# Blocks of 256 rows with four buffers each, in place of blocks of 512 rows with two, in the routed experts of a fused kernel

## The reference, cut to what matters

```python
# h: [8192, 128] tokens after the second layer norm; 8 experts, 2 of them per token
probs = sigmoid(h @ router_w.T + routing_bias)
scores, idx = top_k(probs, 2); scores = scores / scores.sum(-1)     # w: scores at idx
g = silu(einsum('th,ehi->tei', h, gate_w)); u = einsum('th,ehi->tei', h, up_w)
combined = einsum('tei,eih,te->th', g * u, down_w, w)               # routed experts, I = 256
shared = silu(h @ shared_gate.T) * (h @ shared_up.T) @ shared_down.T
x = x + gb * (shared + combined)
```

## Time and profile before

| | |
|---|---|
| time, median of 3 runs | 1456.23 us (1455.55 to 1457.21) |
| the profiled execution: its time, its span in the profile | 1459.87 us, 1458.1 us |
| first load of the block stage issued (SP) | at 1076.5 us of the span |
| last rows of the block stage loaded (SP) | at 1346.0 us |
| first load of the step stage issued (SP) | at 1376.4 us |
| TensorE busy, whole span | 89% |
| TensorE busy from 1100 to 1340 us | 185.7 of 240 us |

### The profile page before, as it was taken

The page is one execution under the profiler, slowest core; times in us unless marked ns, Lnnn a source line. Parts: engine busy times, 40 slices in busy tenths (PEclk is TensorE's granted clock), DMA queues, the critical chain, the costliest instruction groups (busy, mean ns, idle before and its releaser), DMA issues.

```text
span 1458.1 us, 38072 instructions
## 1 busy us (share of the span) xinstructions
PE 1298.9 (89%) x10935; PEld 1072.5 (74%) x10935; DVE 1094.8 (75%) x3120; ACT 812.4 (56%) x2061; POOL 927.0 (64%) x1426
## 2 busy tenths in 40 slices
PE   6999999999999999999999999999138767787796
PEld 5888788888888788888878888787027656676686
DVE  8888889898898988989898998987133433433387
ACT  5666666666666666666666676665023333333342
POOL 3444776867677686776867677676725555555555
PEclk9999999999999999999999999999559988989898
DMA  8902020202112020220202112020224434443154
GB/s 240 259 7 81 2 96 0 95 16 78 40 55 95 6 89 20 75 90 5 95 15 80 34 61 95 4 92 23 103 81 125 130 114 125 122 124 117 50 168 144
DMA packets 94721, 118.46 MB, mean 81 GB/s; under 512 B 9668, under 2 KB 60535, under 8 KB 94672
## 3 DMA queue, kind: packets, MB, share of 16 engines
q1 hardware_dynamic: 85584, 100.93, 22.1%
q0 software_dynamic: 9088, 16.94, 3.5%
HBM read 50.13 MB, written 61.08 MB: 76 GB/s over the span
## 4 chain that ended last, share of the span: by engine, by line
PE 50%; DVE 22%; issue 13%; SPq 7%; POOL 2%; DMA 2%; DVEq 1%; ACT 1%; another core or an unknown queue 1%; POOLq 0%; ACTq 0%
PE head_banks L1394 10%; PE bank L1405 8%; PE bank L1415 6%; DVE pairs L1048 5%; PE bank L1318 5%; PE bank L1319 5%; PE bank L1320 5%; DVE pairs L1044 4%; DVE A L1070 3%; DVE pairs L1053 2%; SPq L384 2%; PE bank L1356 2%; PE bank L1357 2%; PE bank L1358 2%; DVE xn L887 1%
## 5 line engine op out<-in xcount | busy, mean ns | idle before, releaser
L635 POOL DMA_INDIRECT y_dram<-pairs,y_row x156 | 155.0, 994 | 147.3 <-issue 124.9
L1318 PE MATMUL bank<-h_hi,big 128*128 128x256 f32 x768 | 237.2, 309 | 3.4 <-DVE h_lo L895 2.8
L1044 DVE TENSOR_TENSOR_SCAN pairs<-pairs 128x128 f32<-128x128 f32 x512 | 232.2, 494 | 4.4 <-issue 1.7
L1394 PE MATMUL head_banks<-pairs 64*128 64x128 f32 x2048 | 225.9, 297 | 5.3 <-DVE A L1070 3.2
L1405 PE MATMUL bank<-A,shared 128*64 128x256 f32 (+1 forms) x2048 | 223.0, 339 | 0.0
L1048 DVE TENSOR_TENSOR_SCAN pairs<-pairs,cap 128x128 f32<-128x128 f32 x512 | 219.8, 469 | 0.0
L1319 PE MATMUL bank<-h_lo,big 128*128 128x256 f32 x768 | 216.8, 282 | 0.0
L1320 PE MATMUL bank<-h_hi,big 128*128 128x256 f32 x768 | 216.4, 282 | 0.0
L463 POOL TENSOR_SCALAR_AFFINE_SELECT A<-A 128x256 f32<-128x256 f32 x256 | 113.7, 444 | 154.5 <-ACT A L744 153.4
L1394 PEld LDWEIGHTS head_banks<-pairs 64*128 64x128 f32 x2048 | 155.6, 186 | 62.6 <-issue 42.5
L1070 DVE COPY_PREDICATED A<-causal,head_banks 128x384 f32<-128x384 int32 x256 | 150.2, 587 | 63.4 <-PE head_banks L1394 62.2
(11 more groups left out here) (193 smaller groups left out, 2816.3 us busy)
## 6 DMA issues: line engine op xcount, KB each, us to landing
rows_dram<-pad_row SPq DMA_DIRECT2D x17, 2080.0 KB, 8.2
pairs<-rows_dram SPq DMA_DIRECT2D x39, 260.0 KB
pairs<-y_dram SPq DMA_DIRECT2D x16, 512.0 KB, 3.8
pairs<-in_L_ffn_gate_w_dram SPq DMA_DIRECT2D x39, 128.0 KB
pairs<-in_L_ffn_up_w_dram SPq DMA_DIRECT2D x39, 128.0 KB
pairs<-in_L_ffn_down_w_dram SPq DMA_DIRECT2D x39, 128.0 KB
token_rows<-new_rows SPq DMA_DIRECT2D x16, 260.0 KB, 2.3
mod_rows<-mod_rows_dram SPq DMA_DIRECT2D x32, 128.0 KB, 3.2
```

Source lines behind the costliest of these rows:

```text
L635: g.indirect_dma_start(y_dram, bass.IndirectOffsetOnAxis(ap=y_row[:, u, n:n + 1], axis=0), y_out[:, u, n, :], None, bounds_check=TOKENS * ...
L1044: v.tensor_tensor_scan(F[:, par, cols], ga_t[:, par, cols], ga_t[:, par, cols], 1.0, ALU.mult, ALU.min)
L1318: t.matmul(dst, hi, m_hi, start=True, stop=False)
L1394: last = t.matmul(S[:, h, c * P:(c + 1) * P], keys[rows, :], queries[rows, :], start=True, stop=True)
```

## The change

The routed experts' rows are cut into blocks of 256 rows, of which there are 2 * 8192 / 256 + 7 = 71. Every tile that a block loads or stores (`erows`, `ew_in`, `ed_in`, `y_out`, `y_known`, `y_row`) has four buffers, each with a semaphore of its own. The split weights, the split rows and PSUM keep two (`half` in the code). SP's loads run further ahead: rows, gate and up of block i+6 are issued where before it was i+2, down of block i+4 where it was i+1. To make room, `erows` and `ed_in` move into `ga_all`, which is not used by then. GpSimd issues two scatters per block. The loops over blocks are written out four blocks at a time. The step stage still has 512 tokens a step. Some semaphores of other parts are merged, to free eight for the new buffers.

```diff
-BLOCKS = TOP * TOKENS // STEP + E - 1
+BLOCK = 256
+BT = BLOCK // P
+RING = 4
+BLOCKS = TOP * TOKENS // BLOCK + E - 1
...
+        after = ga_all[:, :, :].rearrange("p b d -> p (b d)")
+        erows = after[:, 0:RING * BT * ROW].rearrange("p (u n c) -> p u n c", u=RING, n=BT)
+        ed_in = after[:, 3072:4096].rearrange("p (u i d) -> p u i d", u=RING, i=IT)
...
+        TURNS = (BLOCKS - 3) // RING
+
+        def unit(k, j):
+            return k * RING + j, j % RING, j % 2, k + j // RING
+
+        def begun(turn):
+            return not (isinstance(turn, int) and turn == 0)
...
-            def load_rows(i, u):
-                if not (isinstance(i, int) and i < 2):
-                    alone(s_hx, i - 1)
-                    alone(s_yr, i - 1)
+            def load_rows(k, j):
+                i, u, _, turn = unit(k, j)
+                if begun(turn):
+                    alone(s_hx, i - (RING - 1))
+                    alone(s_yr, i - (RING - 1))
...
-            def load_ahead(i, u):
-                load_rows(i + 2, u)
-                load_gate_up(i + 2, u)
-                load_down(i + 1, 1 - u)
...
+            with sp.Fori(0, TURNS - 1) as k:
+                for j in range(RING):
+                    load_rows(k, j + RING + 2)
+                    load_gate_up(k, j + RING + 2)
+                    load_down(k, j + RING)
...
-                for n in range(ST):
+                for n in range(BT):
                     g.indirect_dma_start(y_dram, bass.IndirectOffsetOnAxis(ap=y_row[:, u, n:n + 1], axis=0),
                                          y_out[:, u, n, :], None, bounds_check=TOKENS * TOP - 1,
                                          oob_is_err=False).then_inc(s_ysc[u], 16)
...
-                if not (isinstance(k, int) and k == 0):
-                    alone(s_ysc[u], k * 64)
+                if begun(turn):
+                    alone(s_ysc[u], turn * 16 * BT)
                 v.tensor_copy(y_row[:, u, :], y_known[:, u, :]).then_inc(s_id, 1)
...
+            def turn_of_blocks(k):
+                for j in range(RING):
+                    rows_transposed(k, j + 2)
+                    gate_up_block(k, j + 1)
+                    down_block(k, j)
```

More of the change, by code:

```diff
@@ L239, in block_kernel @@
         s_tab, s_blk = sem("table_step"), sem("table_ready")
-        s_rin, s_win, s_din, s_ysc, s_yin = ([sem(f"{n}_{u}") for u in range(2)] for n in (
-            "rows_in", "weights_in", "down_in", "y_scattered", "y_loaded"))
+        s_rin, s_win, s_din, s_ysc = ([sem(f"{n}_{u}") for u in range(RING)] for n in (
+            "rows_in", "weights_in", "down_in", "y_scattered"))
+        s_yin = [sem(f"y_loaded_{u}") for u in range(2)]
         s_hx, s_ehh, s_ehl, s_ewh, s_ewl = (sem(n) for n in (
@@ L384, in expert, with load_gate_up @@
                 return sp.value_load(block_i[0:1, 1, ds(i, 1)], min_val=0, max_val=E - 1)
-            def load_rows(i, u):
-                if not (isinstance(i, int) and i < 2):
-                    alone(s_hx, i - 1)
-                    alone(s_yr, i - 1)
[L390 to L395, removed]
+            def load_rows(k, j):
[3 more added lines that the diff above has]
+                    alone(s_yr, i - (RING - 1))
+                row = sp.value_load(block_i[0:1, 0, ds(i, 1)], min_val=0, max_val=ROWS - BLOCK)
+                sp.dma_start(erows[:, u, :, :], rows_dram[ds(row, BLOCK), :].rearrange("(p n) c -> p n c", p=P)).then_inc(s_rin[u], 16)
+            def load_gate_up(k, j):
+                i, u, _, turn = unit(k, j)
+                if begun(turn):
+                    alone(s_ewl, i - (RING - 1))
                 e = expert(i)
@@ L398, in load_gate_up, with load_down @@
                 sp.dma_start(ew_in[:, u, I:2 * I], up_w[ds(e, 1), :, :].rearrange("e h i -> h (e i)")).then_inc(s_win[u], 16)
-            def load_down(i, u):
-                if not (isinstance(i, int) and i < 2):
-                    alone(s_dn, i - 1)
+            def load_down(k, j):
+                i, u, _, turn = unit(k, j)
+                if begun(turn):
+                    alone(s_dn, i - (RING - 1))
                 e = expert(i)
                 sp.dma_start(ed_in[:, u, :, :], down_w[ds(e, 1), :, :].rearrange("e (i p) d -> p (e i) d", p=P)).then_inc(s_din[u], 16)
[L406 to L409, removed]
-            def load_ahead(i, u):
-                load_rows(i + 2, u)
-                load_gate_up(i + 2, u)
-                load_down(i + 1, 1 - u)
[L416 to L425, removed]
+            for i in range(RING):
+                load_rows(0, i)
+                load_gate_up(0, i)
+                if i >= 1:
+                    load_down(0, i - 1)
+            load_down(0, RING - 1)
+            for i in (RING, RING + 1):
+                load_rows(0, i)
+                load_gate_up(0, i)
+            with sp.Fori(0, TURNS - 1) as k:
[3 more added lines that the diff above has]
+                    load_down(k, j + RING)
+            for j in range(3):
+                if j < 1:
+                    load_rows(TURNS - 1, j + RING + 2)
+                    load_gate_up(TURNS - 1, j + RING + 2)
+                load_down(TURNS - 1, j + RING)
+            for u in range(RING):
+                sp.wait_ge(s_ysc[u], 16 * BT * len(range(u, BLOCKS, RING)))
             sp.wait_ge(s_dn, BLOCKS)
@@ L616, in _ @@
                 with pool.Fori(0, B) as b:
-                    alone(s_fmv, b + 1)
-                    g.tensor_scalar(veps[:, :], mv[:, :, 1], EPS, None, ALU.add).then_inc(s_fve, 1)
-                    alone(s_fve, b + 1)
+                    alone(s_fmv, b * 2 + 2)
+                    g.tensor_scalar(veps[:, :], mv[:, :, 1], EPS, None, ALU.add).then_inc(s_frs, 1)
+                    alone(s_frs, b * 2 + 1)
                     g.tensor_tensor(rstd[:, :], veps[:, :], neg_half[:, 0:CHUNKS], ALU.pow).then_inc(s_frs, 1)
@@ L637, in scatter_y @@
                                          oob_is_err=False).then_inc(s_ysc[u], 16)
[L639 to L642, removed]
+            with pool.Fori(0, TURNS) as k:
+                for j in range(RING):
+                    scatter_y(k, j)
+            for j in range(3):
+                scatter_y(TURNS, j)
             pool.wait_ge(s_gb, 16)
@@ L803, in high_h_shared, with silus, copy_y_out @@
                 a.activation(eh_hi[:, u, :], h_all[:, ds(j * STEP, STEP)], ACT.Copy).then_inc(s_ehh, 1)
[L805 removed]
+            def silus(v, width):
                 for i in range(IT):
                     sc.wait_ge(s_g, v * 2 + i + 1)
[L808 to L810 removed]
+                    a.activation(silu[:, i, 0:width], GU[i][0][:, 0:width], ACT.Silu).then_inc(s_silu, 1)
+            def copy_y_out(k, j):
+                v, u, half, turn = unit(k, j)
@@ L811, in copy_y_out @@
                 sc.wait_ge(s_dn, v + 1)
[L812 to L838, removed]
+                if begun(turn):
+                    sc.wait_ge(s_ysc[u], turn * 16 * BT)
+                a.activation(y_out[:, u, :, :], DN[half][:, 0:BT * D].rearrange("p (n d) -> p n d", n=BT), ACT.Copy).then_inc(s_yo, 1)
@@ new lines, in _ @@
+            for j in range(2):
+                high_weights(0, j)
+                high_h(0, j)
+            silus(0, BLOCK)
+            def turn_of_blocks(k):
+                for j in range(RING):
+                    high_weights(k, j + 2)
+                    high_h(k, j + 2)
+                    silus(k * RING + j + 1, BLOCK)
+                    copy_y_out(k, j)
+            turn_of_blocks(0)
+            with sc.Fori(1, TURNS) as k:
+                turn_of_blocks(k)
+            high_weights(TURNS, 2)
@@ L913, in _ @@
                 last = v.tensor_scalar(mod[:, k, :], ps, float(k % 2), None, ALU.add)
-            last.then_inc(s_mod, 1)
+            last.then_inc(s_cm, 1)
             dve.wait_ge(s_rows_ps, 1)
@@ L1227, in gate_times_up, with y_rows, y_rows_out @@
                     alone(s_u, m * 2 + i + 1)
-                    v.tensor_tensor(act[:, u, i, :], GU[i][1][:, :], silu[:, i, :], ALU.mult).then_inc(s_act, 1)
-            def y_rows(m, u, k):
-                alone(s_rin[u], k * 16 + 16)
-                if not (isinstance(k, int) and k == 0):
-                    alone(s_id, m - 1)
+                    v.tensor_tensor(act[:, u, i, 0:width], GU[i][1][:, 0:width], silu[:, i, 0:width], ALU.mult).then_inc(s_act, 1)
+            def y_rows(k, j):
+                m, u, _, turn = unit(k, j)
+                alone(s_rin[u], turn * 16 + 16)
+                if begun(turn):
+                    alone(s_id, m - (RING - 1))
                 v.scalar_tensor_tensor(y_known[:, u, :], erows[:, u, :, D + 1], block_e[:, ds(m, 1)], erows[:, u, :, D],
                                        ALU.not_equal, ALU.add).then_inc(s_yr, 1)
-            def y_rows_out(m, u, k):
+            def y_rows_out(k, j):
+                m, u, _, turn = unit(k, j)
                 alone(s_yr, m + 1)
-                if not (isinstance(k, int) and k == 0):
```

(44 more changed lines are left out.)

204 lines of the change are left out of this document (94 added, 110 removed).

## The result

The changed kernel takes 1514.6 us (median of 4 runs, 1513.9 to 1515.3) where the kernel before took 1455.9 us in the same job: a ratio of 1.0401 [1.0383, 1.0419], 59 us slower. I had forecast slower, at 1559 us. In the profiles the difference is 54 us, since the profiled execution of the kernel before took 1459.87 us, 4 us more than its median. Numbers in fences are start and duration in us unless a sentence says otherwise.

The account below looks back on a forecast made before the run. SP's instruction queue was taken to bound the block stage: 1099 + 64 x 5.65 + 0.9 = 1461.5, plus 18 us, starts the step stage 103 us later; 1456.2 + 103 = 1559 us. Range 1500 to 1620 us.

Parts of the forecast that it names:

- SP's queue paces the changed kernel, so more blocks cost time: Block stage: SP's own instructions set the pace at 5.65 us a block, 71 blocks in place of 39; 75%.
- The first rival: Block stage: the buffers were the bound, so GpSimd paces the new stage at 3.5 us a block, 1422 us; 5%.
- The number: Whole kernel: median of 1559 us, 103 us later than before.
- the second rival: Block stage: SP paces, but short scatter groups don't slow it; 4.22 us a block, 1468 us; 11%.
- the scatters' cost to SP: Block stage: SP's instructions slow beside scatters, 0.71 us per scatter, 1.42 us a block for two.
- SP's quiet work: Block stage: SP's instructions for one block without scatter slowdown, counted as 4.22 us in the changed kernel.
- SP sets the pace of the kernel before, too: Block stage before the change: SP's rows loads every 7.32 us are the stage's pace, with some 12 us of waits.
- the third rival: Block stage: SP's slowdown goes with the block, not the scatters; 6.84 us a block, 1635 us; 8%.
- Other engines, DMA, the step stage: Other engines at most 3.5 us a block, DMA some 150 us hidden in about 400, step stage unchanged at 82 us.
- The signs: New profile: loads 5.65 us apart, SP without waits, 0.7 us pieces beside scatter pairs, TensorE under 77%, cast not released by scatters.

## Why the prediction was right, and where it was off

*SP's queue paces the changed kernel, so more blocks cost time.* Right, and shown in three ways: SP never waits, an unused read costs its full time, and a load moved off SP gives back 89 us. The first rival (GpSimd at 3.5 us a block, 1422 us) is out. Whether SP serves three loads a block or four decides 6% of the time.

In the prediction I held the rule of the Trainium skill ("DMA: Bandwidth & Descriptors", section "Issuing engines are not separate DMA queues"), that starting a DMA is usually small beside the DMA, for refuted by the trace. Taken load by load the trace agrees with it: where SP is quiet, it issues a rows load in 0.33 us, and the rows land 2.1 us after the issue. What does not follow from it is that SP can't be the bound. The four issues are only 1.4 of SP's 4.51 us a block, and the rest is three table reads (not the two I named: the expert is read twice), register operations and waits that are met at once.

*The number* is 44 us off, and 1514.6 us lies outside the 1532 to 1592 us that I gave the forecast itself; it lies in the stated 1500 to 1620 because that range reached towards the second rival.

*The term that was mis-sized is the scatters' cost to SP*: 1.42 us for a pair. It comes to 4.97 - 4.51 = 0.46 us, with the pace measured on the chip of the result and the quiet work on two others; SP's quick instructions have the same medians on both kinds of chip (333 ns for the gate load, 384 for the down load, 0.27 us for the instruction that reads a word of the table). The same kernel with its scatters took 4.55 us a block on a quiet chip, which gives 0.42. I had divided the loss beside four scatters by four. It isn't proportional: the second rival, that a short group hardly slows SP, was nearer. As I had priced it, 1468 us, it missed by as much as the forecast did. With the measured quiet work it comes to 1099 + 64 x 4.51 + 18.9 = 1406.5 for the end of the block stage, 30 us later than before, or 1486 us.

*SP's quiet work* was counted 0.29 us short (4.22, measured 4.51), which hid part of the other error. It made part of it, too: what I did not count as SP's own work in the kernel before I put down to its scatters. With the quiet work 0.29 us longer, four scatters cost an estimated 6.95 - 4.62 = 2.3 us (4.51, and 0.11 more for the loop end of that kernel) and a pair in proportion 1.2, and the pace would again have been forecast at 5.7 us. So the luck is small, and it is the proportion that failed. The measured pace is 0.68 us lower than forecast, 44 us over 64 blocks. SP also issued the rows of block 6 at 1095.0 and not 1099.9, and the end took 17.2 us and not 18: the remaining 5 us of the 49 by which the shift of the block stage's end (54 us, 103 forecast) was off.

*SP sets the pace of the kernel before, too.* Only half right. Where its instructions are slowed, SP is in the loop, but an added read costs about half of its time, so something else holds the pace with it. That it is the scatter group is likely and not shown. ScalarE's late copy of the down product, which the prediction named with the third rival, is another candidate: on the chip of the result it waited like this between 1100 and 1340 us, and on the quiet chip that row is not there.

```profile
ACT pairs L814 <- remote: 43.2, 12, 4.8
```

Where SP is not slowed, the kernel before is paced by TensorE, since half of the scatters can go for a gain of 3 us, and SP waits. There the same change costs 7% and not 4%, as the kernel before gains 70 us from a quiet SP and the changed one only 31.

*Other engines, DMA, the step stage.* Right: under the bound, 45% busy, and 82 us. TensorE was busy some 3.5 us a block, at a mean granted clock of 0.91, where I had counted 2.6 at full clock.

*The signs.* SP without waits, TensorE at 70%, the cast not released by scatters and the step stage came as named. Loads 5.65 us apart and slow pieces beside every pair did not.

*What stays open* is why SP's instructions take 0.7 us beside scatters on some chips. Both chips with a before of over 1450 us show it, the others don't, and the kernels were the same. In the kernel before on the chip of the result, all 84 such instructions (0.60 to 0.76 us, from 1076 to 1345 us) began while scatters were going out or within 1.3 us after, and none began between 1076 us and the first scatter at 1094 us. But no run on such a chip left the scatters out, so that they cause it there rests on the two being side by side in time.

## What to carry to other kernels

A queue that only starts loads has a price per block, here 4.5 us for four loads, three table reads and the waits, and smaller blocks multiply it. Add up its small pieces in the chain of waits before splitting work more finely, and read them in a stretch of many blocks, since single stretches put it 0.3 us too low. More buffers help only the engine that waits for a buffer: with 512 rows they gave 0.6%, the best version here, and in the small blocks less than 1%. A load can be moved to an engine that already makes the wait it needs; here that took back nearly all of the loss, but the small blocks stayed 0.6% slower than before.

## What the runs showed of the hardware

The same program took 1384 to 1388 us on three chips and 1451 to 1456 us on two others, a difference of 5%. Nearly all of it lies in the block stage (72 of 76 us), and with it goes a difference in SP's instructions beside indirect DMAs: 0.70 us each on the one kind, 0.02 to 0.38 us on the other. Whether they are its whole cause is not shown. A comparison of two kernels across chips of both kinds would have meant nothing; even their ratio on one chip moved from 1.040 to 1.070. The cost of the slowdown also depends on how many scatters come in a row: by the estimates above, four in a row cost SP some 2.3 us a block, two 0.46.
